# A graph-attention and mixture-of-experts kernel: a new order of the expert blocks, and weight folds in split halves

## What is computed

```python
q = layernorm(x) @ Wq.T + bq
k = key @ Wk.T + bk
v = value @ Wv.T + bv
s = (q @ k.T) / sqrt(4096) * adj
s = where(abs(s) < 1e-5, -1e9, s)
x = x + softmax(s) @ v @ Wm.T + bm

g = softmax(layernorm(x) @ Wg + bg)             # 8 experts
vals, idx = top_k(g, 2); vals = vals / sum(vals)
y = layernorm(x)
out = x + sum over the 2 chosen experts e of vals_e * (y @ We[e].T + be[e])
```

## Time and profile before

| | us |
|---|---|
| median of 3 executions | 1859.15 (1856.37 to 1859.7) |
| the profiled execution | 1850.15 |
| its span, first to last instruction | 1848.4 |
| TensorE busy in the span | 1804.1 (98%) |
| VectorE busy | 1179.6 (64%) |
| ScalarE busy | 735.1 (40%) |
| POOL busy | 239.9 (13%) |

### The profile page before, as it was taken

How to read it: one execution, slowest core, us unless ns; L and a number is a source line. 1 busy time by engine, 2 the same in 40 slices (tenths; PEclk the granted TensorE clock), 3 DMA queues, 4 the chain that set the end, 5 groups by cost and what they waited for, 6 DMA issues and landing times.

```text
span 1848.4 us, 32928 instructions
## 1 busy us (share of the span) xinstructions
PE 1804.1 (98%) x8730; PEld 849.5 (46%) x8730; DVE 1179.6 (64%) x3111; ACT 735.1 (40%) x1429; POOL 239.9 (13%) x276
## 2 busy tenths in 40 slices
PE   8999999999999999999999999999999999899994
PEld 4544444444444444444444444444444444444552
DVE  2788866666666666666677666666666663554452
ACT  1444443444444434444443333334443333333432
POOL 1000000011000000000000000000000000244545
PEclk9999999999999999999999999999999999999998
DMA  6355556767767676767777555555556567998976
GB/s 205 115 182 182 170 137 149 166 150 172 167 159 173 162 167 157 165 153 168 172 157 185 138 138 135 136 136 136 144 135 147 136 172 153 260 250 199 179 126 86
DMA packets 428395, 296.63 MB, mean 160 GB/s; under 512 B 319025, under 2 KB 335409, under 8 KB 428338
## 3 DMA queue, kind: packets, MB, share of 16 engines
q1 hardware_dynamic: 389714, 230.36, 50.9%
q0 software_dynamic: 16736, 38.35, 10.7%
q10 hardware_dynamic: 21888, 27.27, 4.9%
HBM read 152.68 MB, written 67.72 MB: 119 GB/s over the span
## 4 chain that ended last, share of the span: by engine, by line
PE 82%; DMA 10%; issue 3%; POOLq 1%; DVE 1%; SPq 1%; ACT 1%; POOL 0%; DVEq 0%; ACTq 0%
PE ps L1409 15%; PE ps L1411 15%; PE ps L1410 15%; PE ps L1512 12%; PE ps L1513 11%; PE ps L1514 11%; DMA out<-val_region,tok_ids 8%; PE ps L1418 2%; DMA slots<-work,slots_u 1%; POOLq L682 1%; PE ps L1456 1%; DMA val_region<-in_WmT 0%; DVE work L1359 0%; PE ps L1522 0%; POOL out L690 0%
## 5 line engine op out<-in xcount | busy, mean ns | idle before, releaser
L1409 PE MATMUL ps<-key_region,work 128*128 128x512 f16 (+1 forms) x1336 | 507.6, 380 | 3.0 <-DVE work L1359 2.4
L1411 PE MATMUL ps<-key_region,work 128*128 128x512 f16 (+1 forms) x1336 | 507.5, 380 | 0.0
L1410 PE MATMUL ps<-key_region,work 128*128 128x512 f16 (+1 forms) x1336 | 507.4, 380 | 0.0
L1512 PE MATMUL ps<-val_region,work 128*128 128x512 f16 x1024 | 388.6, 379 | 3.7 <-DMA work<-work 2.6
L1513 PE MATMUL ps<-val_region,work 128*128 128x512 f16 x1024 | 388.6, 380 | 0.0
L1514 PE MATMUL ps<-val_region,work 128*128 128x512 f16 x1024 | 388.5, 379 | 0.0
L765 ACT ACTIVATE work<-work 128x512 f32<-128x512 f32 x256 | 161.4, 631 | 568.3 <-DVE work L1051 568.0
L1051 DVE SCALAR_TENSOR_TENSOR work<-ps,r_cur,work 128x512 f32<-128x512 f32 x256 | 191.7, 749 | 148.3 <-PE ps L1411 133.0
L1073 DVE TENSOR_TENSOR work<-work 128x512 f16<-128x512 f32 x256 | 176.2, 689 | 76.0 <-ACT work L778 75.9
L1061 DVE CUSTOM_DVE_ANT_0 work<-work 128x512 f32<-128x512 f32 x256 | 177.3, 693 | 51.4 <-DVE work L1058 51.4
L773 ACT ACTIVATE work<-work,exp_bias 128x512 f32<-128x512 f32 x256 | 181.4, 709 | 60.4 <-DVE exp_bias L1069 54.6
(11 more groups left out here) (165 smaller groups left out, 1563.0 us busy)
## 6 DMA issues: line engine op xcount, KB each, us to landing
work<-in_adj SPq DMA_DIRECT2D x256, 256.0 KB, 2.9
val_region<-slots SPq DMA_DIRECT2D x58, 257.0 KB, 5.0
work<-in_valueT SPq DMA_DIRECT2D x8, 1024.0 KB, 6.7
work<-in_x SPq DMA_DIRECT2D x8, 1024.0 KB, 5.3
work<-in_keyT SPq DMA_DIRECT2D x8, 1024.0 KB, 5.4
q_scratch<-work SPq DMA_DIRECT2D x8, 1024.0 KB, 5.0
work<-q_scratch SPq DMA_DIRECT2D x32, 256.0 KB, 2.7
work<-in_x SPq DMA_DIRECT2D x32, 256.0 KB, 3.0
```

Of the source, the lines that this page charges most:

```text
L1409: nc.tensor.matmul(bank, st[0], mv[0], start=(k == 0), stop=False)
L1410: nc.tensor.matmul(bank, st[0], mv[1], start=False, stop=False)
L1411: last = nc.tensor.matmul(bank, st[1], mv[0], start=False, stop=(k == n - 1))
L1512: nc.tensor.matmul(bank, st[0], mv[0], start=first, stop=False)
```

## The change

It has two parts.

1. **Order of the blocks.** A list says which half each step belongs to: 27 blocks of half 0, 27 of half 1, then 12 pairs. `add_block` waits for s-1, s-2, s-3 only where that step is of the same half (`beside`). The wait for all earlier adds at the first pair goes. POOL's scatters move: tile 30 after adds 3 and 4, tile 31 after adds 6 and 7.
2. **Folds.** All four weights are loaded in pieces, one after another, and the six small transfers stand behind them. ScalarE and VectorE split each piece into halves (16 instructions each), and both folds and all bias rows are made from the halves in three float16 matmuls each: 48 and 48 for the folds, 12 for `g_row`, 1 and 12 for `c_row`, 40 narrow ones for `u_col` and `c0`. VectorE's part now waits for the small transfers between the split of Wq, Wk and that of Wv, WmT, and it reads the bias rows after it has normalized the first group (`bias_rows`).

```diff
-    TURN = 16
-    LEAD = 31
+    LEAD, PAIRS = 27, 12
+    OF_HALF = [0] * LEAD + [1] * LEAD + [0, 1] * PAIRS
...
+            def beside(self, back):
+                return self.has(back) and OF_HALF[self.first - back] == self.h
...
-            for o in range(KC):
-                for dst, src in ((wq_raw, Wq), (wk_raw, Wk)):
-                    sp.dma_start(dst[:, o, :], src[o * P:(o + 1) * P, :]).then_inc(wqk_loaded[o], 16)
+            for pairs, loaded in ((((wq_raw, Wq), (wk_raw, Wk)), wqk_loaded), (((wv_raw, Wv), (wmT_raw, WmT)), wvm_loaded)):
+                for o in range(KC):
+                    for dst, src in pairs:
+                        sp.dma_start(dst[:, o, :], src[o * P:(o + 1) * P, :]).then_inc(loaded[o], 16)
...
-            for dst, src, loaded in ((wv_raw, Wv, wvm_loaded), (wmT_raw, WmT, wvm_loaded)):
-                sp.dma_start(dst, src.rearrange("(k p) d -> p k d", p=P)).then_inc(loaded, 16)
...
-                for back in (BEHIND // 2,) if st.middle else range(1, BEHIND):
-                    if st.has(back):
+                for back in range(1, BEHIND):
+                    if st.beside(back):
                         pool.wait_ge(y_added[(st.first - back) % RING], first + (st.added(back) - 16))
...
-                if st.first in (5, 6):
-                    scatter_row(T - 2, 1, int(st.first == 6))
-                if st.first in (11, 12):
-                    scatter_row(T - 1, 1, int(st.first == 12))
+                if st.first in (3, 4):
+                    scatter_row(T - 2, 1, int(st.first == 4))
+                if st.first in (6, 7):
+                    scatter_row(T - 1, 1, int(st.first == 7))
             pool.wait_ge(x1_stored, 16 * T)
             pool.wait_ge(tables_done, 2)
-            for back in range(1, BEHIND):
-                pool.wait_ge(y_added[(LEAD - back) % RING], Step(LEAD - back).added(0))
...
+            def split_weights(pairs, loaded):
+                for o in range(KC):
+                    act.wait_ge(loaded[o], 32)
+                    for dst, src in pairs:
+                        nc.scalar.activation(dst[:, 0, o, :], src[:, o, :], ACT.Copy, scale=WS).then_inc(w_hi, 1)
...
+            def split_weights(pairs, first):
+                for o in range(KC):
+                    for i, (dst, src) in enumerate(pairs):
+                        dve.wait_ge(w_hi, first + 2 * o + i + 1)
+                        nc.vector.scalar_tensor_tensor(dst[:, 1, o, :], src[:, o, :], WS, dst[:, 0, o, :],
+                                                       ALU.mult, ALU.subtract).then_inc(w_lo, 1)
+            split_weights(((wq, wq_raw), (wk, wk_raw)), 0)
             dve.wait_ge(b_loaded, 16 * 6)
...
+            split_weights(((wv, wv_raw), (wmT, wmT_raw)), 2 * KC)
...
             spread(0)
             normalize(0)
+            bias_rows()
             project(0)
...
+            def fold(first, left, right):
+                for o in range(KC):
+                    pe.wait_ge(w_lo, 2 * first + 2 * o + 2)
+                    for i in range(KC):
+                        bank, col = ps[:, first + i, :], slice(i * P, (i + 1) * P)
+                        nc.tensor.matmul(bank, left[:, 0, o, col], right[:, 0, o, :], start=(o == 0), stop=False)
+                        nc.tensor.matmul(bank, left[:, 0, o, col], right[:, 1, o, :], start=False, stop=False)
+                        last = nc.tensor.matmul(bank, left[:, 1, o, col], right[:, 0, o, :], start=False, stop=(o == KC - 1))
+                        if o == KC - 1:
+                            last.then_inc(fold_mm, 1)
+            fold(0, wq, wk)
+            fold(KC, wv, wmT)
```

More of the change, by code:

```diff
@@ L68, in graph_attention_moe_kernel @@
     TABLE_STEPS = 16
[L69 removed]
+    assert TOKS % RING == 0 and len(OF_HALF) == SEQ and LEAD + PAIRS == BLOCKS and (T % HALVES) == 0
     PIECES = 4
@@ L102, in graph_attention_moe_kernel @@
         wq_raw, wk_raw, wv_raw, wmT_raw = (raw[:, i] for i in range(4))
+        w_split = val_region[:, 8 * KC * D:16 * KC * D].rearrange("p (w h k d) -> p w h k d", w=4, h=2, k=KC)
+        wq, wk, wv, wmT = (w_split[:, i] for i in range(4))
         taken = [0]
@@ L262, in graph_attention_moe_kernel @@
         wqk_loaded = [sem(f"wqk_loaded{o}") for o in range(KC)]
-        wvm_loaded = sem("wvm_loaded")
+        wvm_loaded = [sem(f"wvm_loaded{o}") for o in range(KC)]
+        w_hi = sem("w_hi")
+        w_lo = sem("w_lo")
+        b_scaled = sem("b_scaled")
+        b_hi = sem("b_hi")
+        u_read = sem("u_read")
         b_loaded = sem("b_loaded")
@@ L392, in has @@
             def has(self, back):
-                return self.later or self.first >= back
+                return self.first >= back
+            def beside(self, back):
+                return self.has(back) and OF_HALF[self.first - back] == self.h
             def ahead(self):
-                return Step(self.first + AHEAD, self.turn)
-        def lead_steps():
-            return [Step(s) for s in range(LEAD)]
-        def turn_steps(j, later=False):
-            return [Step(LEAD + i, j, later) for i in range(TURN)]
-        def tail_steps():
-            return [Step(s) for s in range(SEQ - LEAD, SEQ)]
+                return Step(self.first + AHEAD)
+        steps = [Step(s) for s in range(SEQ)]
+        lead, rest = steps[:LEAD], steps[LEAD:]
         block = ctx.enter_context(nc.Block())
@@ L598, in _ @@
             sp.wait_ge(padded[1], 16 * E)
-            for st in turn_steps(0) + tail_steps():
+            for st in rest:
                 load_block(st)
@@ L922, in _ @@
                     gap_exponent(T - 1)
-            for st in turn_steps(0):
-                block_hi(st.ahead())
-                block_gate(st)
-            for st in tail_steps():
+            for st in rest:
                 if st.first + AHEAD < SEQ:
@@ L1394, in _ @@
             dve.wait_ge(tables_done, 2)
-            for st in turn_steps(0):
-                block_lo(st.ahead())
-                block_bias(st)
-            for st in tail_steps():
+            for st in rest:
                 if st.first + AHEAD < SEQ:
@@ L1439, in _ @@
-            pe.wait_ge(fold_out, 3)
-            for j in range(KC):
-                exact(ps[:, 2, j:j + 1], [(wk_raw[:, o, j * P:(j + 1) * P], bq_col[:, o:o + 1]) for o in range(KC)])
-            exact(ps[:, 2, KC:KC + 1], [(x_wide[0][:, o, :], bq_col[:, o:o + 1])
-                                        for o in range(KC)]).then_inc(fold_mm, 1)
+            nc.tensor.matmul(ps[:, 1, :], ones[0:1, :], bm_row[:, :], start=True, stop=False)
+            for o in range(KC):
+                nc.tensor.matmul(ps[:, 1, :], bv_wide[:, 0, o, :], wmT[:, 0, o, :], start=False, stop=False)
+                nc.tensor.matmul(ps[:, 1, :], bv_wide[:, 0, o, :], wmT[:, 1, o, :], start=False, stop=False)
+                last = nc.tensor.matmul(ps[:, 1, :], bv_wide[:, 1, o, :], wmT[:, 0, o, :], start=False, stop=(o == KC - 1))
@@ new lines, in _ @@
+            last.then_inc(fold_mm, 1)
+            pe.wait_ge(fold_out, 3)
+            for j in range(KC + 1):
+                for o in range(KC):
+                    hi, lo = ((wk[:, h, o, j * P:(j + 1) * P] if j < KC else bk_wide[:, h, o, :]) for h in range(2))
+                    nc.tensor.matmul(ps[:, 2, 2 * j:2 * j + 2], hi, bq_split[:, o, :], start=(o == 0), stop=False)
+                    last = nc.tensor.matmul(ps[:, 2, 2 * j:2 * j + 1], lo, bq_split[:, o, 0:1], start=False, stop=(o == KC - 1))
@@ L1618, in _ @@
             pe.wait_ge(tables_done, 2)
-            for st in turn_steps(0):
-                turn_block(st.ahead())
-                multiply_block(st, True)
-            for st in tail_steps():
+            for st in rest:
                 if st.first + AHEAD < SEQ:
                     turn_block(st.ahead())
-                multiply_block(st, False)
+                multiply_block(st)
 def kernel(x, adj, L0_gnn_key, L0_gnn_value, L0_gnn_Wq, L0_gnn_bq, L0_gnn_Wk, L0_gnn_bk, L0_gnn_Wv, L0_gnn_bv,
```

112 lines of the change are left out of this document (52 added, 60 removed).

## The result

| | before | after |
|---|---|---|
| median of 5 executions, us | 1857.06 (1851.99 to 1859.7) | 1842.89 (1840.46 to 1845.68) |
| ratio | 1 | 0.9933 [0.9913, 0.9953] |
| the profiled execution, us (its span) | 1850.15 (1848.4) | 1845.68 (1843.7) |
| end of TensorE's last matmul to the end, us | 23.1 | 12.3 |

By the profiled executions alone the gain is 4.5 us, since that of before is a low one: 83 executions of the old kernel that ran beside the experiments, in five groups, have medians from 1855.1 to 1856.9. So the profiles tell where the time went, and the medians how much. In the interval of the ratio the gain is 8.7 to 16.2 us.

A forecast was written before the change was run, and what follows sets the result against it. TensorE was taken to bound the kernel, with POOL's adds having a part in the block stage's losses. Folds -3.4 and blocks -4.2 sum to -7.6, from 1859.15 to 1851.5 us; range 1843 to 1859 for eight in ten.

The forecast's parts named there:

- four rivals: Clock breaks at each drain: 1869, 0.08; biases at 24.7: 1855.2, 0.12; order does nothing: 1855.7, 0.12; scatters free: 1846, 0.10.
- Folds, -3.4 forecast: Weight folds before attention: the first turning of x moves from 55.87 to 52.5, a gain of 3.4 us.
- bound of 18.2: Small transfers in the folds: earliest landing if only their issue at 15.0 counts; the folds' gain would be 6.2 us.
- Second fold: TensorE in the folds: starts at 26.9, at half clock after 8.7 us idle, and ends at 39.0, over 4 us later.
- In time by 0.7: End of the folds: VectorE is ready at 51.8, before TensorE's first turning at 52.5.
- Blocks, -4.2 forecast: Block stage, following POOL's adds: add 77 goes at 1835.8 against 1839.98, 4.2 us earlier.
- Scatters +1.0: POOL early in the block stage: the moved scatters gain nothing; add 13 at 1650.3 against 1649.28.
- bound of +8: Scatters in the block stage: upper bound, if a landing takes 15 us as add 3's did.
- Steps 27 to 53: Half 1 alone, on POOL: 26 adds with 7 new starts at 7.0 us take 84.2 us.
- Steps 54 to 77: Pairs at the end, on POOL: 44.4 us plus five new starts, 16.5 us in all; add 77 at 1835.8.
- TensorE's margin: End of the block stage: TensorE would allow add 77 at 1831.3, so POOL is last by 4.5 us.
- I take the difference over: Last step of the sum: the median's 9.0 us above the profiled execution is kept, giving 1859.15 - 7.6 = 1851.5.

The follow-up runs named there:

- e1: Old kernel with only the folds changed, the order of blocks and scatter places as before; 1849.57 us, ratio 0.9965.
- e7: Changed kernel with the six small transfers issued ahead of Wv and WmT, VectorE's order left alone; 1834.87 us, ratio 0.9889.
- e2: Old kernel with only the order of blocks, its waits and the scatters' places changed, folds as before; 1848.52 us, ratio 0.9962.
- e3: Changed kernel with POOL's scatters back at their old places, after adds 5, 6, 11 and 12; 1841.63 us, ratio 0.9926.
- e6: Changed kernel with both edits, e4's later bias work and e3's old scatter places; 1830.70 us, ratio 0.986.
- e4: Changed kernel with VectorE's bias work moved behind the split of Wv and WmT, nothing else; 1832.14 us, ratio 0.9873.
- e5: The old kernel run again, unchanged, for a second profile; median 1856.63 us, ratio 1.0, profiled execution 1859.00 us.
- e12: Old kernel with expert 3's weights loaded before the block loop and experts 4 to 7 in steps 4 to 7; 1848.23 us, ratio 0.9956.

## Why the prediction was right, and where it was off

**The sign and the two causes: right.** Both parts gain, alone and together, each by about half, and of the cases named the likeliest is the one that the profile shows. All four rivals fell: the clock broke once in the stage and not at each drain (0.87 in one stretch, below), the biases came at 21.90 and not at 24.7, the order gave its part, and the scatters were not free.

**Folds, -3.4 forecast; -2.2 at the first turning in after's profile, -3.2 in e1's.** (By the timeline's 55.71 the forecast itself would be -3.2.) Point by point:

- First matmul 6.33 (6.1). The fold ended near 19.66 for 18.2, since the half clock lasted from 6.33 to 12.28 and cost 3.0 us, not 1.7.
- Biases 21.90 (21.0), by another way than argued. The last small transfer was to be issued at 15.0 and was at 19.38: the eight weight issues took SP 5.6 us and not 3.8, and from the first small one to the last it was 9.2 (3.84 for bv_col alone), 2.5 more than was taken over from before. It landed 2.5 after its issue. The value halfway between two bounds was near by luck; the bound of 18.2 could never have come, since the issue itself was later.
- The Trainium skill (DMA: Bandwidth & Descriptors, "Queues, rings and completion order") says that descriptors are consumed in ring order on each engine. The prediction took from it that the small transfers can't overtake the weights, so that they land late. No run here shows such an effect: between e7 and after the last small transfer is issued 7.3 us later (12.12 and 19.38) and VectorE goes on 7.0 us later (14.92 and 21.90), so the late issue explains all of it.
- Second fold 27.86 (26.9), at half clock as said, which cost 2.4 for 1.7. Narrow products took 1.0 us (47.0 to 48.0) for the 2.1 forecast: the price taken from weight loads was twice too high.
- "In time by 0.7": TensorE was through with the value tiles near 53.2 and VectorE at 53.40. This cover was gone, and VectorE ended the folds, by 0.3 us.

**Blocks, -4.2 forecast; -6.6 to -7 by the medians of e2, on the way from add 26 to add 77 -5.2 forecast and -6.4 measured.** The terms under it are further off and cancel in part, which is luck:

- Scatters +1.0: add 13 came at 1650.56, and was forecast at 1646.9 with the folds' gain taken off. The sum followed POOL alone and left out that adds 8 and 9 hold the ring: TensorE lost 12.3 us at turnings 22 and 23. How much of this reaches the end, e3 (against after) and e6 (against e4) tell: 5 us in the profiled executions, 1.3 and 1.4 in the medians. The bound of +8 was for a cause that did not come (a landing after 15 us).
- Steps 27 to 53 took 87.8 us (1691.66 to 1779.43) for 84.2: new starts cost 6.2 to 8.0 us there, 7.5 in the mean, and not 7.0. The timeline puts five of the seven down to ScalarE; in the chain of waits it is for six of them (all but add 47) the landing of the add before, 5.4 to 7.0 us from its issue, and only for add 47 the scaling.
- Steps 54 to 77 took 56.2 for 60.9: new starts cost 4.6, 4.9 and 4.3, and after the third of them no wait is over 1.8 us; five were counted.
- TensorE's margin: forecast were POOL last by 4.5 us, and about 15 us from the last matmul to the end. It was 2.4 and 12.3.

**The size: nearly twice the forecast.** The step that failed is the last one of the sum: "I take the difference over". An execution 5 to 7 us below the usual has lost less somewhere, and what it lost less is no constant of the program. Here it had not met the stall at 1603 (e5, e2), and the new kernel meets it in none of its profiles. So the difference between usual executions is larger than one that is summed against a lucky old one. How often the old kernel meets the stall is not known: one of its two profiles has it, and so has e2's. Against e5 the profiled execution of after is 13.3 us shorter: 2.1 at the first turning, 8.3 by add 4, 4.7 by add 26 (the echo of the scatters gives some back), 12.8 by add 77. Besides, 2.1 of the 8.6 us between forecast and measurement lie in the median taken as base (1859.15, and 1857.06 with two executions more).

**The conditions for being wrong.** The second fold did not start after 30, the adds 27 to 53 took under 90, and the granted clock of the whole stage, 0.97, stayed over 0.95. It fell where the ring stalled TensorE, and was back at once after; windows of the changed kernel:

```profile
1560.00:1640.00 80.00, 73.50 (x383) 37.61 (x381) 43.03 (x155) 23.77 (x40) 23.95 (x21) 0.98 0.94 255
1640.00:1680.00 40.00, 31.41 (x153) 16.62 (x154) 16.55 (x44) 13.44 (x23) 15.79 (x11) 0.87 0.97 220
1680.00:1831.00 151.00, 147.82 (x768) 78.42 (x767) 71.25 (x187) 57.90 (x96) 82.26 (x54) 1.00 0.86 146
```

In the third, with all the new starts of half 1 alone in it, the clock is at 1.00: the drains reached TensorE as turnings late by 0.9 us at most. The Trainium skill (TensorE: Matmul & The Clock Gate, "HAM oscillation") tells of a kernel whose recurring waits for data cost the clock each time. Waits as short as these cost none here, so its case didn't arise; after the one long wait (8.78) the turning ran at half clock, as it says of each such wait.

## What to carry to other kernels

Where an in-order engine does two jobs, put the wait that ends last behind the work that others need first: one call moved in VectorE's order (e4) was worth 10.8 us, three quarters of the whole change. Before a difference is summed against one profiled execution, see how that execution lies among the others, and look in a second profile for the wait that the low one didn't have. And a transfer that many wait for (here a transposing one, and the blocks behind it) can be worth a clear stretch: five bulk loads moved by a few steps (e12) gave the old kernel as much as half of the change.

## What the runs showed that was not expected

- A transposing transfer landed in 3.1 us with nothing beside it, in 11.6 to 20.0 beside adds, block loads and weight loads, and in 6.9 and 8.2 with the weight loads moved off. In the windows of e2 the DMA engines were busy throughout (a share of 1.17) between 1591 and 1600 and moved 59 GB/s:

```profile
1591.00:1600.00 9.00, 4.92 (x24) 2.06 (x21) 4.07 (x16) 3.23 (x5) 2.45 (x3) 0.92 1.17 59
```

- The issue of a transfer costs SP from 0.33 us (`bm`) to 3.84 (`bv`, a 128x4 column of single elements, behind the weights; 1.11 in the kernel before): SP's queue is itself a place where a kernel waits.
- A start after idle cost TensorE from 1.7 us (e4, half clock from 6.31 to 9.7) to 3.0 (after, 6.33 to 12.28), with the same matmuls in both.
- Moved scatters reached TensorE by a detour: POOL, the landing of add 9 (11.3 us of ScalarE's wait), the ring, VectorE, and the turning of a block 5 steps on.
